# Swapping the down and up projections in each unit of an expert stage on one core

## What is computed

```python
shared = jax.nn.silu(xf @ Ws_up) @ Ws_down
aff = xf @ centroids.T
_, idx = jax.lax.top_k(aff + expert_biases, 8)
w = jax.nn.sigmoid(jnp.take_along_axis(aff, idx, axis=1))
w = w / (jnp.sum(w, axis=-1, keepdims=True) + 1e-08)
cw = jnp.zeros((T, E)).at[jnp.arange(T)[:, None], idx].add(w)
h = jax.nn.silu(jnp.einsum('td,edf->etf', xf, W_up))
y = jnp.einsum('etf,efd->etd', h, W_down)
out = shared + jnp.einsum('etd,te->td', y, cw)
```

## Time and profile before

| what | before |
|---|---|
| median of 3 runs | 1024.24 us |
| the runs | 1022.57, 1024.37, 1024.24 us |
| the profiled execution | 1021.6 us |
| its span in the trace | 1019.9 us |
| TensorE busy, share of the span | 946.4 us, 93% |
| VectorE busy | 825.4 us, 81% |
| ScalarE busy | 700.0 us, 69% |
| GpSimd busy | 480.2 us, 47% |
| granted clock of TensorE, mean | 0.956 |

### The profile page before, as it was taken

One profiled execution on the slowest core, in us unless ns is written; L12 is line 12 of the kernel. 1 busy time (PEld: TensorE's weight loads), 2 busy tenths in 40 slices (PEclk: granted clock), 3 DMA queues, 4 the chain that ended last, 5 costly groups with the idle time before them and its releaser, 6 DMA issues.

```text
span 1019.9 us, 20123 instructions
## 1 busy us (share of the span) xinstructions
PE 946.4 (93%) x6082; PEld 754.9 (74%) x6115; DVE 825.4 (81%) x1938; ACT 700.0 (69%) x1394; POOL 480.2 (47%) x550
## 2 busy tenths in 40 slices
PE   3686999999789999999999979999999999999997
PEld 2564998999657677767776657787877777778786
DVE  6888776777778888888887668989898889898865
ACT  3763554555467777877787657777777778777875
POOL 3278782107456565656553404444444444444443
PEclk8765999999779999999999999999999999999999
DMA  8994332222201110110010008493939292939291
GB/s 258 403 386 167 109 95 67 69 66 69 60 24 28 30 29 23 29 33 24 22 32 12 1 16 197 97 210 82 213 76 220 72 222 66 213 76 219 70 228 42
DMA packets 69156, 111.00 MB, mean 109 GB/s; under 512 B 16783, under 2 KB 54706, under 8 KB 64962
## 3 DMA queue, kind: packets, MB, share of 16 engines
q1 hardware_dynamic: 64080, 100.72, 37.8%
q0 software_dynamic: 4384, 8.99, 2.8%
q10 hardware_dynamic: 594, 0.09, 0.0%
HBM read 70.90 MB, written 38.86 MB: 108 GB/s over the span
## 4 chain that ended last, share of the span: by engine, by line
PE 74%; DVE 16%; ACT 4%; issue 3%; DMA 1%; SPq 1%; DVEq 0%; POOLq 0%; ACTq 0%
PE ps L2494 6%; PE ps L2476 5%; PE ps L2477 5%; PE ps L2478 5%; PE ps L2495 5%; PE ps L2496 5%; PE ps L2199 3%; DVE nm L1919 3%; PE ps L2307 3%; PE ps L2329 3%; PE ps L2301 3%; PE ps L2346 3%; PE ps L2177 2%; PE ps L2179 2%; PE ps L2178 2%
## 5 line engine op out<-in xcount | busy, mean ns | idle before, releaser
L927 POOL TENSOR_TENSOR hl<-h,hh 128x512 fp32r<-128x512 f32 x128 | 166.8, 1303 | 247.8 <-ACT hh L1238 247.8
L1238 ACT ACTIVATE hh<-h 128x512 fp32r<-128x512 f32 (+1 forms) x264 | 165.4, 627 | 43.8 <-DVE h L2004 41.2
L2004 DVE TENSOR_TENSOR h<-ps,cwB 128x512 f32<-128x512 f32 x192 | 130.8, 681 | 31.0 <-ACT ps L1227 28.1
L1919 DVE TENSOR_REDUCE nm<-ps 128x4 f32<-128x512 f32 (+1 forms) x128 | 116.3, 951 | 38.0 <-PE ps L2329 35.9
L1227 ACT ACTIVATE ps<-ps 128x512 f32<-128x512 f32 x192 | 111.6, 581 | 25.6 <-PE ps L2478 24.8
L2476 PE MATMUL ps<-xh,wh 128*128 128x512 f32 x256 | 103.0, 403 | 0.0
L2494 PE MATMUL ps<-hh,wh 128*128 128x512 f32 x256 | 102.3, 400 | 0.6 <-POOL hl L927 0.6
L2011 DVE TENSOR_TENSOR hl<-h,hh 128x512 fp32r<-128x512 f32 (+1 forms) x136 | 95.9, 705 | 8.4 <-ACT hh L1238 8.1
L2495 PE MATMUL ps<-hl,wh 128*128 128x512 f32 x256 | 100.0, 390 | 0.0
L2477 PE MATMUL ps<-xl,wh 128*128 128x512 f32 x256 | 100.0, 390 | 0.0
L2478 PE MATMUL ps<-xh,wl 128*128 128x512 f32 x256 | 99.9, 390 | 0.0
(11 more groups left out here) (367 smaller groups left out, 2671.4 us busy)
## 6 DMA issues: line engine op xcount, KB each, us to landing
cwB<-cwd SPq DMA_DIRECT2D x32, 1536.0 KB, 13.8
ys<-zfill SPq DMA_DIRECT2D x13, 1536.0 KB, 22.6
cwd<-cwS SPq DMA_DIRECT2D x64, 96.0 KB
xb<-xs SPq DMA_DIRECT2D x72, 64.0 KB
ys<-yb SPq DMA_DIRECT2D x72, 64.0 KB
x_res<-in_L_attn_x_dram SPq DMA_DIRECT2D x4, 512.0 KB, 6.6
wst<-in_L_ffn_W_up_dram SPq DMA_DIRECT2D x32, 64.0 KB, 2.1
wst<-in_L_ffn_W_down_dram SPq DMA_DIRECT2D x32, 64.0 KB, 1.9
```

What stands on the lines that cost most here:

```text
L927: pool.tensor_tensor(hl4[:, slot(u), :], h4[:, slot(u), :], hh4[:, slot(u), :].bitcast(F32), op=ALU.subtract).then_inc(u_hlp, 1)
L1238: act.activation(hh4[r, slot(u), :], h4[r, slot(u), :], ACT.Copy).then_inc(u_hh, 1)
L1919: ins = dve.tensor_reduce(nm[:, u, 4 * g:4 * g + 4], o, axis=AX.X, op=ALU.max, negate=True)
L2004: dve.tensor_tensor(h4[:, slot(u), :], first, second, op=ALU.mult).then_inc(u_h, 1)
```

## The change

In each unit TensorE does the down projection of unit u - 4 first, then the up projection of u and its spreading matmul, which has a function of its own now. The work put in at some units still comes last. Nothing else is changed: the matmuls, the waits in front of each, the semaphores, the buffers and the other engines' orders are the same.

```diff
@@ -2476,6 +2476,8 @@
                 pe.matmul(o, hi, xh4[:, p, :], start=True, stop=False)
                 pe.matmul(o, hi, xl4[:, p, :], start=False, stop=False)
                 pe.matmul(o, lo, xh4[:, p, :], start=False, stop=True).then_inc(u_up, 1)
+
+            def e_spread(t, p, u):
                 if u > 0 and not broadcast_unit(u):
                     wait_bank(pe, t, "spread", u)
                     pe.matmul(bank[spread_bank(u)][:, :], selr[:, 2 * u - 2:2 * u, :].rearrange("p e f -> p (e f)"), cwT[:, p, :],
@@ -2506,11 +2508,12 @@
 
             def pe_tile(t, p, before, N, S):
                 for u in range(NU):
-                    e_up(t, p, u)
                     if u >= LAG:
                         e_down(t, p, u - LAG)
                     elif before is not None:
                         e_down(before[0], 1 - p, NU + u - LAG)
+                    e_up(t, p, u)
+                    e_spread(t, p, u)
                     if before is None:
                         last_attended(u)
                     if u == 7 and before is not None:
```

## The result

The changed kernel takes 1038.97 us (median of 4 runs, 1038.39 to 1039.32), the kernel before 1023.57 us beside it (4 runs, 1022.57 to 1024.37). The ratio is 1.0152, 95% interval 1.0139 to 1.0165: 15.4 us slower. The forecast was 1043 us with a range of 1034 to 1056.

The account below looks back on a forecast made before the run. The last stage was taken to run at TensorE's pace. Losses of 2.65 + 1.6 + 12.95 + 1.3 + 0.68 = 19.2 us on 1024.24 gave 1043 us, 1.9% slower; own range 1037 to 1051, 8-in-10 range 1034 to 1056.

Parts of the forecast that it names:

- the room: Time a low half is ready before its down projection's place: 1.02 us at unit 13, tile 7; the change takes 1.36.
- The calm sum: Tile 7, without routing steps: odd units' down projections 9 to 29 lose 0.115 us each, 1.3 us in all.
- D(9) and D(13): Down projections of units 9 and 13, calm part of tiles 0 to 6: 2.65 and 1.6 us lost in all.
- The cost of a late release: At a down projection's weight load on TensorE: a late release loses its lateness less 0.11 us.
- the weights-ahead rival: Waiting down projections have weights loaded already, so each losing wait costs 0.11 us less: 1034 us; chance 0.06.
- The busy stretch: Units 14 to 29 of tiles 0 to 6, VectorE full with routing: net 1.85 us a tile, 12.95 in all.
- The additive rival: Releases move with TensorE, each down projection pays its own shortage: 5.4 us a tile, 1064 us; chance 0.11.
- catching up once a tile: TensorE falls back once a tile, then stays behind the others, which keep their times: 1035 us; chance 0.13.
- The faster rival: Down projections fill bank-wait gaps in units 0 to 8, with no new wait: 1016 us; chance 0.04.
- No change: New waits in the last stage only replace the bank waits and the down projections' existing waits: 1024 us; chance 0.03.
- the end's 0.68: End of the last tile: the last up projection comes three matmuls later, 0.68 us.

Follow-up runs that it names:

- e1: The changed kernel with the down projection of unit u - 5 in place of u - 4; ratio 1.0007 to the kernel before.
- e2: The kernel before, up projection first, with the down projection of unit u - 3 in place of u - 4; ratio 1.0160.
- e5: The changed kernel with GpSimd computing half of each odd low half, used twice; ratio 0.9977 to the kernel before, 1085.3 us on a slower chip.
- e16: The kernel before with its lag of four kept for units 0 to 12's down projections, five for 13 to 32's; ratio 0.9953, 1017.5 us.
- e3: The kernel before with the down projection first in units 0 to 16 only; ratio 1.0058.
- e14: The kernel before with the changed order in the last tile only; ratio 1.0021, last stage 2.8 us longer.
- e4: The kernel before with the down projection first in units 17 to 32 only; ratio 1.0105.
- e6: The kernel before with GpSimd computing half of each odd low half, used twice; ratio 0.9903, 1077.8 us on a slower chip.

## Why the prediction was right

**That TensorE sets the pace and the room is what counts: right.** e1 and e2 show that the change is one of distance, e5 that giving the odd ones back their room takes away 10 of the 17.5 us, e16 that more room in the busy stretch alone gains 4.7.

**The calm sum: right.** Forecast 1.3 us for tile 7, measured 1.15 to U(32) (1.32 from U(7) on). It doesn't settle at 0.115 per odd unit, as I took it, but goes to and fro: 0.24 at one odd down projection, 0.02 at the next, which is 0.13 on average; no even one waits before U(32). D(9) and D(13): 0.26 and 0.25 in tile 1, 0.48 for D(9) in tile 3, against 0.23 and 0.49.

**The cost of a late release: right.** D(20) in tile 2 was 0.93 late and lost 0.83; D(13) in tile 7 0.32 and 0.20 (the second matmul at 1003.96, due at 1003.76). Both are lateness less 0.10 to 0.12. The load stands with its matmul at 1003.62, as in the earlier trace rows, so the weights-ahead rival (1034 us) is out. The Trainium skill's rule of the reorder window (TensorE: Matmul & The Clock Gate, "Architectural detail: the array is 16× 32×32, not 1× 128×128") isn't contradicted, but no row here shows a load that passes a wait.

**The busy stretch: right in sum.** Stepped through for tile 1, measured in tile 1 (what the distance between ups shows over 1.36):

| down projection | 15 | 17 | 18 | 19 | 20 | 21 | 23 | 24 | 25 | 29 | sum |
|---|---|---|---|---|---|---|---|---|---|---|---|
| forecast | 0.03 | 0.20 | 0.13 | 0.17 | 0.85 | 0.28 | 0 | 0 | 0.25 | 0.57 | 2.48 |
| measured | 0.03 | 0.23 | 0.12 | 0.19 | 0.83 | 0.28 | 0.03 | 0.21 | 0.20 | 0.39 | 2.51 |

D(24), for which I took nothing, loses 0.21, and D(29) loses 0.18 less than I took, so the sum agrees better than its parts. The order of before loses 0.50 from D(15) to D(26) in tile 1, and 0.15 to 0.17 more on D(29) (from U(0) to U(1) it is 1.56 us in tile 3, and 1.39 in the changed kernel). Together that is near the 0.63 that I took off, and net 1.86 a tile against 1.85.

That losses shadow each other is what D(29) shows: 0.86 in e3 and 0.84 in e14, with little late before it, 0.39 here. So does tile 7, where every second odd one loses next to nothing. The additive rival (1064; by the terms that it names its 5.4 a tile should have been 5.2 at most, 1063) is out by the result, and so is catching up once a tile (1035), since tile 7, which has nothing to catch up with, still loses 1.15.

**The faster rival: out.** The spreading matmul's wait did fall by 2.6 us, as that rival said it might, which doesn't come near to the 25.6 us by which the down projections' waits grew. *No change* is out by the result.

**What was wrong by some us.** The sum was 19.2, the profiled spans differ by 16.8 and the medians by 15.4 (the profiled execution before was 2.0 us under its median, the one after 0.6). I had forecast L2496's waits for GpSimd at 25 to 35 us in 70 to 80 times; they are 23.8 in 59, in part because in tile 7 every second odd one is all but in time. Those for VectorE are 11.6, near the 10 that I forecast. Of the terms: the end's 0.68 was counted though the start takes it in (tile 7 and the end have 1.15 in place of 1.98), which e14 shows. Tile 4 has 1.69 in place of 2.57. It is the first tile of the hardware loop's second round. VectorE stands idle for 2.7 us there, ahead of the first low half (814.21), and for 3.0 in the changed kernel; in e1 and e4 the profile finds nothing that this pause (2.8 and 2.9 us) waits for. From U(2) to U(7) tile 4 is 1.15 us longer than tile 3 in the order of before and 0.27 in the changed one, so part of the loss is hidden behind this pause. Why it is there wasn't tested. The stage began 0.7 us sooner in the execution after, which is not the change's.

## What to carry over

When one engine alternates between producing and consuming, read the order as a distance: swapping the two halves of a step takes a whole step from every dependency or gives one, and a one-line reordering is a change of lag. Measure the room at each consumer (its place less the release), subtract what falls out, and step through the result, since a wait gives room to those behind it. To price one cause by taking it out, do so in both kernels: without the reciprocal both gained nearly the same, and the change cost what it had. And a length of 400 us with a low clock at its start can hide 1 or 2 us, so measure it from a place where the clock is the same. A longer distance pays where the producers are late and costs where it holds a buffer, so it can be set by stretch: four units where places are tight and five where VectorE is full gained 0.5%.

## What the runs showed of the hardware that was not expected

GpSimd's step slows some of VectorE's. In e6 GpSimd's share is halved, and three routing steps on VectorE that nothing else touched are shorter. Before (all executions of a line, min/median/max in ns; L1852 compares two tensors of SBUF, L1822 copies, L1814 multiplies by a tensor of factors):

```profile
L1852 DVE TENSOR_TENSOR g<-mr,bi x8: 424/931/1041, 600.0 to 943.7; 128x256 f32<-128x256 f32 x8
...
L1822 DVE COPY cs<-cwh x7: 958/964/970, 651.9 to 956.0; 128x64 f32<-128x64 f32 x7
...
L1814 DVE TENSOR_TENSOR g<-g,s x7: 822/830/934, 648.8 to 952.9; 128x64 f32<-128x64 f32 x7
```

and in e6:

```profile
L1852 DVE TENSOR_TENSOR g<-mr,bi x8: 413/421/481, 664.5 to 1002.1; 128x256 f32<-128x256 f32 x8
...
L1822 DVE COPY cs<-cwh x7: 410/410/411, 715.8 to 1013.3; 128x64 f32<-128x64 f32 x7
...
L1814 DVE TENSOR_TENSOR g<-g,s x7: 260/275/369, 713.2 to 1010.8; 128x64 f32<-128x64 f32 x7
```

By the medians 0.51, 0.55 and 0.55 us less. It is not the chip: e1, on the chip of e6 and with GpSimd's whole step, has 0.94, 0.97 and 0.83. Nor is it a fixed price, but one of how the steps fall together: in e16 L1852 takes 0.61 us, in the changed kernel L1814 takes 1.06, both beside whole steps of GpSimd. The GPSIMD Engine Reference of the Trainium skill, section "1. Specifications", says that GpSimd's interfaces to SBUF are shared with VectorE, with contention where VectorE has two SBUF inputs or runs in a two-port mode. L1852 and L1814 have two SBUF inputs, and the numbers agree; in which mode L1822 runs no run shows. I had taken VectorE's durations as fixed.

This is part of why e6 gained more than I expected. Of the 8.3 us that it gains from U(3) on, 4.6 are the waits of down projections (with those of D(29)), 0.6 is the end, and 3.1 lie in units 3 to 6, where I had counted nothing. There the spreading matmul waits for its bank 5.5 us in the order of before and 1.8 in e6, and VectorE's norm step ahead of it (L1769, the 16 of the hardware loop's tiles) takes 5.9 us in place of 8.1. The routing steps can't have given more than the waits that they caused, since TensorE has no others there. The two causes were not run apart.
